# Expert slots of a mixture-of-experts layer: gate and up run with the weights in the array, from copied weights

## The reference

```python
logits = xf @ router_w
top_idx = jnp.argmax(logits, axis=-1)
top_score = jax.nn.sigmoid(jnp.max(logits, axis=-1))
def body(acc, ew):
    g, u, d, e = ew
    w = jnp.where(top_idx == e, top_score, 0.0)[:, None]
    xe = xf * w
    hmid = jax.nn.silu(xe @ g) * (xe @ u)      # g, u: 256 x 512
    return (acc + hmid @ d, None)              # d: 512 x 256
shared = jax.nn.silu(xf @ sh_gate) * (xf @ sh_up) @ sh_down
```

## Time and profile before

| | |
|---|---|
| median of 3 runs (range) | 1096.91 us (1096.4 to 1099.36) |
| profiled execution, its own time | 1098.5 us |
| span from its first to its last instruction | 1096.6 us |
| PE busy over the span | 93% |
| DVE, ACT, POOL busy over the span | 62%, 42%, 34% |
| slot stage, first down (843.83) to last but one (1079.56) | 235.73 us for 37 slots |

### The profile page before, as it was taken

One profiled execution on the slowest core, in us unless ns is written; L12 is line 12 of the kernel. 1 busy time (PEld: TensorE's weight loads), 2 busy tenths in 40 slices (PEclk: granted clock), 3 DMA queues, 4 the chain that ended last, 5 costly groups with the idle time before them and its releaser, 6 DMA issues. The chain is left out here.

```text
span 1096.6 us, 17525 instructions
## 1 busy us (share of the span) xinstructions
PE 1023.3 (93%) x5522; PEld 534.0 (49%) x5522; DVE 675.0 (62%) x1694; ACT 457.5 (42%) x685; POOL 371.7 (34%) x498
## 2 busy tenths in 40 slices
PE   7998899999997999999998999999977999999995
PEld 4554344444443444444433666666634555555553
DVE  4788888888885888888742555555541333333332
ACT  2552466666764666666664122221111222222221
POOL 7992332222221222222221133333363322233232
PEclk9999899999998999999998999999998999999998
DMA  7786444444446444444004472221522112111211
GB/s 274 188 235 147 65 68 69 70 64 70 69 126 99 64 65 65 62 66 69 11 12 152 136 228 73 74 78 39 194 94 79 59 64 68 62 61 65 67 59 39
DMA packets 78276, 100.06 MB, mean 91 GB/s; under 512 B 28048, under 2 KB 64400, under 8 KB 74864
## 3 DMA queue, kind: packets, MB, share of 16 engines
q1 hardware_dynamic: 63904, 70.48, 31.2%
q0 software_dynamic: 5712, 15.93, 3.8%
q10 hardware_dynamic: 8576, 12.58, 3.4%
HBM read 65.86 MB, written 32.70 MB: 90 GB/s over the span
## 5 line engine op out<-in xcount | busy, mean ns | idle before, releaser
L1034 ACT ACTIVATE probs<-scores_ps 128x1024 f32<-128x1024 f32 (+3 forms) x384 | 290.7, 809 | 140.8 <-PE scores_ps L960 138.8
L301 DVE TENSOR_REDUCE maxima<-max_ps 128x1 f32<-128x512 f32 (+2 forms) x352 | 231.8, 688 | 44.8 <-PE max_ps L259 22.7
L259 PE MATMUL max_ps<-k_stack,q_stack 96*128 96x512 bf16 (+3 forms) x768 | 222.4, 331 | 13.1 <-DMA q_stack<-q_parts 7.0
L1125 POOL TENSOR_SCALAR_AFFINE_SELECT probs<-probs 128x512 f32<-128x512 f32 x128 | 81.7, 638 | 323.4 <-ACT probs L1034 323.4
L960 PE MATMUL scores_ps<-q_stack,k_stack 99*128 99x512 bf16 (+3 forms) x768 | 184.7, 330 | 2.3 <-PEq L359 1.6
L980 PE MATMUL out_ps<-probs,v_ones 128*32 128x512 f32 (+3 forms) x1536 | 164.3, 500 | 2.2 <-POOL probs L1125 1.8
L296 DVE CUSTOM_DVE_ANT_0 masked_out<-max_ps,mask_wide 128x384 bf16<-128x384 f32 (+1 forms) x256 | 151.5, 622 | 20.6 <-PE max_ps L259 18.0
L259 PEld LDWEIGHTS max_ps<-k_stack,q_stack 96*128 96x128 bf16 x768 | 74.6, 97 | 162.3 <-DVE maxima L296 56.5
L1406 ACT ACTIVATE silu<-gate_ps 128x512 f32<-128x512 f32 x71 | 42.4, 597 | 235.1 <-PE gate_ps L1325 138.3
L960 PEld LDWEIGHTS scores_ps<-q_stack,k_stack 99*128 99x128 bf16 x768 | 69.8, 99 | 52.8 <-issue 8.3
L1476 DVE TENSOR_TENSOR hidden<-silu,up_ps 128x512 f32<-128x512 f32 x39 | 26.8, 688 | 104.2 <-PE up_ps L1335 104.2
(11 more groups left out here) (169 smaller groups left out, 1272.9 us busy)
## 6 DMA issues: line engine op xcount, KB each, us to landing
k_stack<-k_parts SPq DMA_DIRECT2D x96, 128.0 KB, 4.5
q_stack<-q_parts SPq DMA_DIRECT2D x96, 128.0 KB, 7.5
q_parts<-parts SPq DMA_DIRECT2D x32, 192.0 KB, 3.2
k_parts<-parts SPq DMA_DIRECT2D x32, 192.0 KB, 3.2
rows_in<-expert_rows SPq DMA_DIRECT2D x39, 136.0 KB
sums_in<-expert_sums SPq DMA_DIRECT2D x39, 128.0 KB, 2.0
x_t<-in_x_cols SPq DMA_DIRECT2D x8, 512.0 KB, 10.9
heads_rows<-heads_out SPq DMA_DIRECT2D x32, 128.0 KB, 1.7
```

What stands on the lines that cost most here:

```text
L259: last = nc.tensor.matmul(part, self.q_stack[:ROWS, u.slot, h0 + k, t * P:(t + 1) * P], self.k_stack[:ROWS, u.slot, h0 + k, chunk * BLOCK: ...
L301: nc.vector.tensor_reduce(self.maxima[:, u.slot, chunk, h0:h0 + heads, t], self.bank("piece", u.i, n)[:, :heads * keys].rearrange("p (h k) ...
L1034: nc.scalar.activation(probs[:, s % RING, 2 * pair:2 * pair + 2, n0:], scores_ps[:, pair, :, n0:], ACT.Exp).then_inc(exp_done, 1)
L1125: nc.gpsimd.affine_select(out=tile, in_=tile, compare_op=ALU.is_ge, fill=0.0, base=0, pattern=[[0, GROUP], [1, P]], channel_multiplier=-1) ...
```

## The change

Gate and up are turned round: a 128 x 128 piece of the weights is the operand held in the array, the 128 transposed rows are streamed, and the results come out with the inner features on the partitions, as `expert_down` wants them. `turn_hidden`, `keep_hidden` and the buffer `hidden` are gone; `times_up` writes `hidden_t`. For each slot ACT copies the expert's gate weights (128 x 1024 f32) into `gate_now` and DVE the up weights into `up_now`, rings of two in the memory of two tiles of the shared stage (`heads_in` and `res`). PE reads the copies, so gate and up need no register; down still does. `turn_rows(j + 2)` stands ahead of `expert_up(j + 1)`. `ROW_RING` is 4.

```diff
-    ROW_RING, SUM_RING = 3, 3
+    ROW_RING, SUM_RING = 4, 3
...
+        gate_now = f.heads[:].rearrange("p o t g e -> p o (t g e)").rearrange("p o (c n) -> p o c n", c=DC)
+        up_now = f.res[:].rearrange("p o t d -> p o (t d)").rearrange("p o (c n) -> p o c n", c=DC)
...
             def expert_gate(j):
-                e = pe.value_load(owner_i[0:1, j:j + 1], min_val=0, max_val=EXPERTS - 1)
                 pe.wait_ge(rows_t_kept, j + 1)
                 pe.wait_ge(silu_made, TILES + j - 1)
-                for c in range(DC):
-                    last = nc.tensor.matmul(gate_ps[:, j % 2], rows_t[:, j % 2, c * P:(c + 1) * P], gate_w[:, e, c],
-                                            start=(c == 0), stop=(c == DC - 1))
+                pe.wait_ge(gate_copied, j + 1)
+                for n in range(IC):
+                    for c in range(DC):
+                        last = nc.tensor.matmul(gate_ps[:, j % 2, n * P:(n + 1) * P],
+                                                gate_now[:, j % 2, c, n * P:(n + 1) * P],
+                                                rows_t[:, j % 2, c * P:(c + 1) * P],
+                                                start=(c == 0), stop=(c == DC - 1))
                 last.then_inc(gate_done, 1)
...
             def expert_down(j):
                 e = pe.value_load(owner_i[0:1, j:j + 1], min_val=0, max_val=EXPERTS - 1)
-                pe.wait_ge(hidden_t_kept, j + 1)
+                pe.wait_ge(hidden_made, TILES + j + 1)
...
                 expert_gate(j + 1)
-                turn_hidden(j)
+                turn_rows(j + 2)
                 expert_up(j + 1)
-                turn_rows(j + 2)
                 expert_down(j)
...
+            def copy_gate(j):
+                if j >= SLOTS:
+                    return
+                e = act.value_load(owner_i[0:1, j:j + 1], min_val=0, max_val=EXPERTS - 1)
+                if j >= 2:
+                    act.wait_ge(gate_done, TILES + j - 1)
+                stand(act, act_stood)
+                nc.scalar.copy(gate_now[:, j % 2], gate_w[:, e]).then_inc(gate_copied, 1)
...
                 if nxt is None:
+                    act.wait_ge(tables_made, 1)
+                    act.wait_ge(f.heads_turned, BLOCKS)
+                    act.wait_ge(keep["weights_in"], 16 * 2 * EXPERTS)
+                    copy_gate(0)
                     keep_rows(0)
                     keep_rows(1)
                     make_silu(BLOCKS, 0)
+                    copy_gate(1)
...
             for j in range(SLOTS):
                 if j + 1 < SLOTS:
                     make_silu(BLOCKS, j + 1)
-                keep_hidden(j)
                 keep_rows(j + 2)
+                copy_gate(j + 2)
...
             def times_up(i, t):
                 if isinstance(i, int) and i == BLOCKS:
-                    wait(dve, hidden_turned, t - 1)
-                    out = hidden[:, t % 2]
+                    dve.wait_ge(down_done, TILES + t - 1)
+                    out = hidden_t[:, t % 2]
...
+            def copy_up(j):
+                if j >= SLOTS:
+                    return
+                e = dve.value_load(owner_i[0:1, j:j + 1], min_val=0, max_val=EXPERTS - 1)
+                if j >= 2:
+                    dve.wait_ge(up_done, TILES + j - 1)
+                stand(dve, dve_stood)
+                nc.vector.tensor_copy(up_now[:, j % 2], up_w[:, e]).then_inc(up_copied, 1)
...
                 if nxt is None:
                     times_up(BLOCKS, 0)
+                    copy_up(1)
...
                 if last:
                     make_tables()
+                    dve.wait_ge(tables_made, 1)
+                    dve.wait_ge(keep["weights_in"], 16 * 2 * EXPERTS)
+                    copy_up(0)
...
                     times_up(BLOCKS, j + 1)
                 if j >= 1:
                     normalise(j - 1)
+                copy_up(j + 2)
                 add_sum(j)
```

More of the change, by code:

```diff
@@ L1168, in feed @@
     dve_stood, pool_stood = f.dve_stood, f.pool_stood
-    heads_turned, xf_made, xf_t_kept, placed = f.heads_turned, f.xf_made, f.xf_t_kept, f.placed
+    xf_made, xf_t_kept, placed = f.xf_made, f.xf_t_kept, f.placed
     row_made, token_made = f.row_made, f.token_made
@@ L1176, in feed @@
         silu = b.sb("silu", [P, 2, INNER])
-        hidden = b.sb("hidden", [P, 2, INNER])
         hidden_t = b.sb("hidden_t", [P, 2, INNER])
@@ L1217, in feed @@
         gate_done, silu_made, hidden_made = b.sem("gate_done"), b.sem("silu_made"), b.sem("hidden_made")
[L1218 removed]
+        down_done = b.sem("down_done")
         down_in = b.sem("sh_down_in")
@@ L1221, in feed @@
         block = ctx.enter_context(nc.Block())
+        gate_copied, up_copied, act_stood = b.sem("gate_copied"), b.sem("up_copied"), b.sem("act_stood")
+        gate_now = f.heads[:].rearrange("p o t g e -> p o (t g e)").rearrange("p o (c n) -> p o c n", c=DC)
+        up_now = f.res[:].rearrange("p o t d -> p o (t d)").rearrange("p o (c n) -> p o c n", c=DC)
         def slot_down(j):
@@ L1295, in down @@
                 last.then_inc(down_done, 1)
[L1297 to L1303, removed]
             def turn_rows(j):
@@ L1331, in expert_up @@
                     return
-                e = pe.value_load(owner_i[0:1, j:j + 1], min_val=0, max_val=EXPERTS - 1)
                 pe.wait_ge(hidden_made, TILES + j - 1)
-                for c in range(DC):
-                    last = nc.tensor.matmul(up_ps[:, j % 2], rows_t[:, j % 2, c * P:(c + 1) * P], up_w[:, e, c],
-                                            start=(c == 0), stop=(c == DC - 1))
+                pe.wait_ge(up_copied, j + 1)
+                for n in range(IC):
+                    for c in range(DC):
+                        last = nc.tensor.matmul(up_ps[:, j % 2, n * P:(n + 1) * P],
+                                                up_now[:, j % 2, c, n * P:(n + 1) * P],
+                                                rows_t[:, j % 2, c * P:(c + 1) * P],
+                                                start=(c == 0), stop=(c == DC - 1))
                 last.then_inc(up_done, 1)
```

## The result

The changed kernel took **1067.48 us** (median of 4, 1065.43 to 1070.05) against 1098.05 for the one before (1096.4 to 1099.36): ratio 0.972, 95% interval 0.9698 to 0.9742. The profiled execution took 1067.94 us, its span 1066.1. Forecast: 1064, range 1056 to 1080.

What follows compares the result with a forecast made beforehand. PE's chain of waits was taken to bound the slot stage; the slot falls from 6.37 to 5.47 us (1.76 + 0.22 + 1.76 + 1.73), 33.3 us over 37 slots, ends cancelling, giving 1064 us, range 1056 to 1080.

Steps and rivals of the forecast that it cites:

- The passes: Gate and up: 16 passes of 128 columns each, weight load hidden, 0.110 us a pass; 0.08 us a slot more than before.
- Rivals 1 and 2: Gate and up passes: load not hidden, 1123 us, chance 0.06; or passes 0.12 to 0.13 us, 1076 to 1088, chance 0.09.
- rival 1: Gate and up's 32 passes: load doesn't hide under 128 columns, 0.16 us a pass, 26 us more, 1123; chance 0.06.
- The gap, "all of them or none": Ahead of down: four row buffers remove 0.50 us a slot, or none if down's register load stays exposed.
- PE's sequencer stands at that wait: Row transposes wait for the rows' DMA, so PE can't run ahead and down's register load is late; 0.50 us a slot.
- `turn_hidden` goes: 0.44 us off the chain.: PE's slot chain: dropping the transposes of hidden saves 0.44 us a slot.
- The rows' slack: With four buffers, rows arrive 7.1 us after up's end (T), and the transposes want them at 9.0.
- The copies' cover: ACT's copy done by 2.9 us, DVE's by 2.0 to 3.2, both wanted at 3.7; costed at nothing, slack 0.5 at worst.
- rival 3: DVE's copied up weights become the bound if register load and copy exceed 2.6 us; 1079 at 3.0; chance 0.05.
- The ends: Last block's up copy costs 0, covered by PE's rows wait; first slot loses 0.5 us, last gains 0.5; these cancel.
- Rival 4: Stretch between the stages, with DVE's 22.4 us of "remote" waits, shifts 6 us either way: 1058 or 1070; chance 0.07.

Runs made afterwards that it cites:

- set 2: Four kernels on one chip: kernel before again (1091.72), changed kernel again (1055.97), old operands with four buffers and new order (1067.09), changed kernel with `copy_up(0)` later (1055.12).
- set 3: On one chip: turned operands with three buffers, transposes behind up (1096.84); changed kernel with copies doubled (1069.51), with five buffers (1069.37), unchanged (1068.26); kernel before took 1097.19.
- sets 1 and 2: Two sets of four kernels, each set on one chip with the kernel before, which took 1091.66 in the first and 1091.83 in the second.
- the one run meant for it: Changed kernel with POOL's tail scatters of the sums (`set_sum_tails`) moved behind the last block's own scatters: 1061.22 us, ratio 0.9728 to the kernel before.

## Why the prediction was right, and where it was not

The slot, by its four factors (us a slot, steady):

| | rows behind up | rows ahead of up |
|---|---|---|
| old operands, 3 buffers | 6.37 | not run |
| turned operands, 3 buffers | 6.36 | 7.4 |
| old operands, 4 buffers | 5.82 | 5.82 |
| turned operands, 4 buffers | 5.96 | 5.51 |

- **The passes.** 0.1115 against 0.110 taken: 32 x 0.0015 = 0.05 us a slot, nearly all of 5.51 against 5.47. Over 37 slots it is 1.6 us of the 3.5 between forecast and median; 1.2 more is the later first down, and the rest lies mainly in the median of the kernel before, 1098.05 with the result and 1096.91 when the forecast was made. The load hides, as the transposes in the earlier trace rows said. Rivals 1 and 2 are out, and with rival 1 the ratio from the Trainium skill, page "TensorE: Matmul & The Clock Gate", section "Back-to-back issue gap": by the estimate from it, 81 / 56, 0.108 would have become 0.157, and the trace has 0.1115. (The slot by that estimate is 32 x 0.157 + 1.95 = 6.97, where the prediction has 6.9.)
- **The gap, "all of them or none".** All of it, as forecast, and 0.55 by the run with four buffers against 0.50. But the step that explained it was incomplete. "PE's sequencer stands at that wait" is what the rows show, and the register load behind it is a part of the cost; the prediction didn't ask why the rows were late by just that much in every slot. It had the answer in its hands: it followed the rows from `add_sum` over SP and the transfer for four buffers, and not for three. For three that sum closes on itself and is the slot. So half a microsecond was right as a size, and the fourth buffer as the cure, but the wait for rows isn't a cost beside the work of PE: it fills whatever PE leaves of the round.
- **"`turn_hidden` goes: 0.44 us off the chain."** True only once the round is opened. Alone, with its copies, it is worth 0.01 a slot; with the fourth buffer 0.44 - 0.13 for 32 slower passes = 0.31. The forecast's total stands because all parts came together; that the parts add was not shown by it, and is false with three buffers.
- **The rows' slack.** The prediction had rows at T + 7.1, wanted at T + 9.0. SP issues 3.04 us after T (878.34 to 881.38) and a rows transfer lands 2.1 after its issue on the page, so they are there at T + 5.2: DVE's copy takes 0.69, as the lower of its two bounds nearly said (0.6), and `add_sum` begins at T + 1.8.
- **The copies' cover.** Right for both; rival 3 is out by the run that doubles them.
- **The ends.** `copy_up(0)` cost PE 1.38 us ahead of the third up. That the later rows wait covers it held on the chip of set 2: without the gap PE waits longer, passes at the lower clock follow, and the sums' arrival ends the second slot about where it did. In the first slot up(1) followed the row transposes without a gap (843.28), so the 0.5 lost there wasn't there either. The last slot: its down begins 1.4 us sooner after the one before (1.72 instead of 3.08), and the end gains none of it, since POOL's roots and writes set the end; the 0.5 gained wasn't there. The two terms did cancel, but by being nothing both, which is luck.
- **Rival 4.** It took part beside the main case. The first down came 1.2 later; from the first gate of the last shared block to it there are 3.6 us more than before (794.22 to 845.07 against 796.55 to 843.83), of which 1.4 are the gap ahead of up. The other 2.3 of the 3.6 don't show in the 1.2, since the changed kernel came to that gate earlier in its profile. On a chip without the "remote" waits the ratio of the changed kernel is 0.9665, with them 0.972 and 0.9729, a difference of some 6 us, as much as the rival had allowed.

## What to carry to other kernels

A wait of a quarter or half a microsecond that returns in every iteration is the visible end of something. Follow it back through every engine and queue until it meets itself: if it closes in one iteration, no iteration can be shorter than it, and work taken off the busiest engine turns into a wider gap. The run with the transposes behind up shows a second such round, over ACT instead of SP. PE busy for 96% of a stage didn't exclude that. So try the one-number change (a deeper ring) alone before the large one: here it gave 0.55 of the 0.86 us a slot, and the rewrite's own part appears only behind it.

## What the runs showed of the hardware

- Waits without a named releaser ("remote", on DVE's `total` and ACT's `rows_t`) stand between the stages in the profiles of some sets and not of others, for the same kernel: on DVE 22.4 us before the change and 20.9 after it in the first profiles, 15.0 to 20.9 in the four of set 3, none in the eight of sets 1 and 2; on ACT 20.0 to 21.7, but 6.0 in the kernel before. Each set is one chip, so whether they go with the chip or come and go on one isn't shown. They fall while POOL issues its indirect transfers at its usual pitch (1.27 us, as without them), and SP takes 16.0 us for the four row issues there instead of 4.0. Between set 3, which has them, and set 2 the changed kernel differs by 12.3 us (1068.26 against 1055.97) and the one before by 5.4 (1097.19 against 1091.83). Not all of it is theirs: in its profile of set 3 the changed kernel was 3.0 later already at the first gate of the last shared block (798.71 against 795.68 in set 2). The kernel before loses less because in their absence its first sums are late (its first two slots take 9.87 and 8.46). With the waits no second slot is long: the sums arrive in the meantime. Their cause stays open; the one run meant for it met none.
- Doing work earlier can cost clock: behind 4.22 us of waiting the next passes ran at a granted clock of 0.50 (8 in 3.62 us, later 8 in 1.89 again), behind 2.65 us at 1.00 (1.89).
- A copy of 128 x 1024 f32 within SBUF takes 0.69 us on DVE and 1.05 on ACT; in the slots shown a register load leaves 0.25 to 0.34 us of issue ahead of ACT's copy.
